# Attention's own-chunk products: 64x64 tiles on v where it stands, in place of 128x32 tiles on placed copies of v

## The reference, cut to what matters

```python
x = x + 0.5 * ffn(layernorm(x), w_gate, w_up, w_down)     # FP4 quantised, H=256, I=704
x = x + attn(layernorm(x), Wqkv, bqkv, Wout, bout, gamma, beta)
x = x + 0.5 * ffn(layernorm(x), w_gate, w_up, w_down)

# attn: linear attention, 16 heads of 16
q = (elu(q) + 1 + 1e-4) / sqrt(16);  k = elu(k) + 1 + 1e-4
num = einsum('blhe,blhef->blhf', q, cumsum_l(k v^T))
den = einsum('blhe,blhe->blh',   q, cumsum_l(k)) + 1e-4
out = layernorm((num / den) @ Wout.T + bout) * gamma + beta
```

## Time and profile before

| | |
|---|---|
| median of 3 runs | 2228.23 us |
| span of the profiled execution | 2226.0 us |
| PE busy | 2120.2 us, 95% |
| PEld busy | 1488.7 us, 67% |
| DVE busy | 2060.1 us, 93% |
| ACT busy | 1849.7 us, 83% |
| POOL busy | 1897.2 us, 85% |
| mean granted clock of TensorE | 0.994 of full speed |

### The profile page before, as it was taken

One profiled execution on the slowest core, in us unless ns is written; L12 is line 12 of the kernel. 1 busy time (PEld: TensorE's weight loads), 2 busy tenths in 40 slices (PEclk: granted clock), 3 DMA queues, 4 the chain that ended last, 5 costly groups with the idle time before them and its releaser, 6 DMA issues.

```text
span 2226.0 us, 90845 instructions
## 1 busy us (share of the span) xinstructions
PE 2120.2 (95%) x30384; PEld 1488.7 (67%) x30384; DVE 2060.1 (93%) x5231; ACT 1849.7 (83%) x3880; POOL 1897.2 (85%) x3002
## 2 busy tenths in 40 slices
PE   3899999999999899999999999969999999999998
PEld 1566666666666678888888888855656665666665
DVE  7999999999999689999999999978999999999997
ACT  7888888888888688888888888868888888888884
POOL 6899999999999677888888888868989999999996
PEclk9999999999999999999999999999999999999999
DMA  4765555555556433333333333324655555555555
GB/s 104 128 121 115 116 112 112 116 116 114 113 112 110 81 65 71 72 72 72 72 70 72 72 72 70 72 54 80 114 112 112 113 113 113 112 113 113 113 116 112
DMA packets 740337, 217.67 MB, mean 98 GB/s; under 512 B 670497, under 2 KB 740001, under 8 KB 740257
## 3 DMA queue, kind: packets, MB, share of 16 engines
q1 hardware_dynamic: 740256, 216.68, 48.2%
HBM read 20.38 MB, written 16.78 MB: 17 GB/s over the span
## 4 chain that ended last, share of the span: by engine, by line
DVE 38%; PE 20%; issue 12%; SPq 11%; POOL 11%; DMA 4%; DVEq 2%; ACT 1%; POOLq 0%; ACTq 0%
DVE ffn_y L748 10%; DVE ffn_per_block L717 8%; DVE ffn_hx L710 7%; PE ffn_ps_gu L860 6%; SPq L1028 5%; SPq L1034 4%; POOL ffn_h_hl L790 4%; POOL ffn_h_hl L791 4%; PE attn_ps_qk L1254 3%; DVE ffn_q L744 3%; PE ffn_ps_down L872 3%; DMA attn_xT<-attn_x_hl 3%; SPq L1040 2%; PE attn_ps_num L1293 2%; DVE ffn_scale L723 2%
## 5 line engine op out<-in xcount | busy, mean ns | idle before, releaser
L860 PE MATMUL ffn_ps_gu<-wgu_hi,ffn_xT 128*128 128x512 f16 (+1 forms) x3072 | 737.6, 363 | 17.7 <-DVE ffn_hx L710 7.5
L860 PEld LDWEIGHTS ffn_ps_gu<-wgu_hi,ffn_xT 128*128 128x128 f16 x3072 | 300.8, 98 | 303.6 <-issue 22.0
L806 ACT ACTIVATE ffn_quarter<-ffn_y,offsets 128x960 int16<-128x960 f32 (+2 forms) x264 | 282.6, 1071 | 185.0 <-DVE ffn_y L748 184.9
L860 PE MATMUL ffn_ps_gu<-wgu_lo,ffn_xT 128*128 128x512 f16 (+1 forms) x1536 | 431.0, 362 | 0.0
L872 PE MATMUL ffn_ps_down<-wd_hi,ffn_hT 128*128 128x256 f16 x2816 | 351.1, 273 | 18.9 <-DVE x_sb L737 13.6
L790 POOL TENSOR_TENSOR ffn_h_hl<-ffn_q,ffn_h_scale_hi 128x704 f16<-128x704 f16 x256 | 352.2, 1376 | 12.5 <-DVE ffn_h_scale_lo L754 8.4
L791 POOL TENSOR_TENSOR ffn_h_hl<-ffn_q,ffn_h_scale_lo 128x704 f16<-128x704 f16 x256 | 354.0, 1383 | 0.0
L872 PEld LDWEIGHTS ffn_ps_down<-wd_hi,ffn_hT 128*128 128x128 f16 x2816 | 265.7, 98 | 99.6 <-issue 37.0
L717 DVE TENSOR_REDUCE ffn_per_block<-ffn_hx 128x60 f32<-128x960 f32 (+2 forms) x264 | 298.4, 1130 | 21.3
L748 DVE TENSOR_TENSOR ffn_y<-ffn_hx,ffn_per_block 128x960 f32<-128x960 f32 (+2 forms) x264 | 295.3, 1119 | 0.0
L842 ACT ACTIVATE ffn_odd<-ffn_quarter,offsets 128x960 f16<-128x960 int16 (+2 forms) x264 | 278.7, 1056 | 10.5 <-POOL ffn_shift L783 10.5
(11 more groups left out here) (183 smaller groups left out, 5081.5 us busy)
## 6 DMA issues: line engine op xcount, KB each, us to landing
attn_v_eo<-attn_v_nat SPq DMA_DIRECT2D x512, 34.0 KB, 1.9
x_sb<-in_L_attn_x SPq DMA_DIRECT2D x128, 128.0 KB, 2.5
out<-x_sb SPq DMA_DIRECT2D x128, 128.0 KB, 2.1
ffn_xT<-ffn_x_hl SPq DMA_TRANSPOSE x256, 2.4
ffn_hT<-ffn_h_hl SPq DMA_TRANSPOSE x256, 3.5
attn_xT<-attn_x_hl SPq DMA_TRANSPOSE x128, 2.4
attn_oT<-attn_o_hl SPq DMA_TRANSPOSE x128, 2.4
x_sb<-in_L_ffn_w_gate SPq DMA_DIRECT2D x2, 352.0 KB, 5.0
```

The lines of the kernel that those rows point to most:

```text
L806: nc.scalar.activation(quarter[:, back], y[:, back], ACT.Identity, bias=offsets[:, 0:1], scale=4.0 / HALF_MIN).then_inc(S["quarter"], 1)
L860: last = nc.tensor.matmul(ps_gu[par][:, a:b], xT[par][:, c, :], w[:, k, a:b], start=(n == 0), stop=(n == len(terms) - 1))
```

## The change

The scores are now written with the keys of chunk s at the partitions half(s), where the v of that chunk stands, and even and odd heads lie side by side in the free dimension. The own-chunk product reads v where ScalarE wrote it: contraction over the 64 keys of chunk s, 64 columns of weights (all its queries), 17 moving columns (one head). Both operands and the output of chunk s lie at half(s), so chunk 0 uses the tile of the array at rows and columns 0 to 63, and chunk 1 that at rows and columns 64 to 127. There are again 32 such products per tile. `v_eo`, its four DMAs and all waits on them are gone. `v_nat` gets four buffers in place of two (hence a phase of 0 to 3 in place of the parity), and ScalarE no longer waits for a buffer of it to be free. The 32 products raise a new semaphore `own_done` at their last, and TensorE waits for it before the products with the state; that wait is new.

```diff
 def tensor_step(pe, i, phase):
...
                 ready(pe, "q_feat", tn)
-                placed(pe, tn, oth)
                 ready(pe, "masked", tn)
...
+                pe.sem_inc(S["turn"], 1)
                 for c in range(DC):
-                    for r in range(PAIRS):
-                        for u in range(4):
-                            s, m = u // 2, u % 2
-                            h = c * PAIRS + r % 2 * 2
-                            nc.tensor.matmul(num[quarter(u), r // 2, h:h + 2, :], scores[:, r // 2, c, s, r % 2, quarter(m)], v_eo[oth][:, s, :, c * PAIRS + r, :],
-                                             start=(c == 0 and r % 2 == 0), stop=False, skip_group_check=True)
+                    for g in range(2):
+                        for h in range(PAIRS):
+                            j, a = h // 2, h % 2
+                            for s in range(2):
+                                last = nc.tensor.matmul(num[half(s), g, c * PAIRS + h, :], scores[half(s), g, c, a, j, :], v_nat[(phase - 1) % PHASES][half(s), a, c * PAIRS + g * 2 + j, :],
+                                                        start=(c == 0 and h == 0), stop=False, skip_group_check=True)
+                last.then_inc(S["own_done"], 1)
+                ready(pe, "own_done", tn)
+                pe.sem_inc(S["turn"], 1)
...
-                                last = nc.tensor.matmul(ps_sc[half(a), g, c, s], k_eo[par][half(g), c, s, a], q_rows[par][half(g), c, :, half(s)], start=True, stop=True)
+                                last = nc.tensor.matmul(ps_sc[half(s), g, c, a], k_eo[par][half(g), c, s, a], q_rows[par][half(g), c, :, half(s)], start=True, stop=True)
...
 def sync_step(sp, i, phase):
...
-            if valid(tv, N):
-                ready(sp, "v_nat", tv)
-                sp.sem_inc(S["turn"], 1)
-                freed(sp, "num_done", tv, 2)
-                sp.sem_inc(S["turn"], 1)
-                for s in range(2):
-                    for a in range(2):
-                        sp.dma_start(v_eo[oth][half(a), s, a], v_nat[oth][half(s), a]).then_inc(S["v_eo" + even_odd], 16)
...
 def scalar_step(act, i, phase):
...
-                freed(act, "kv_done", tf, 2)
-                if not (isinstance(tf, int) and tf < 2):
-                    placed(act, tf - 2, oth)
-                nc.scalar.activation(v_nat[oth][:]...
+                nc.scalar.activation(v_nat[(phase + 1) % PHASES][:]...
```

More of the change, by code:

```diff
@@ L79 @@
 ATTN_TURN = 4
+PHASES = 4
 def in_order(eng, step, first, end):
     for i in range(first, end):
-        step(eng, i, i % 2)
+        step(eng, i, i % PHASES)
 def in_turns(eng, step, first, end, turn):
@@ L90, in in_turns @@
         for k in range(turn):
-            step(eng, i + k, (first + k) % 2)
+            step(eng, i + k, (first + k) % PHASES)
 FIRST, DEPTH = 12, 6
@@ L699, in sync_step, with vector_step @@
                 sp.dma_start(out_t[to], x_sb[:, to, :]).then_inc(stored, 16)
-        def vector_step(dve, i, par):
+        def vector_step(dve, i, phase):
+            par = phase % 2
             oth = 1 - par
@@ L878 @@
 ATTN_SEMS = ("sums", "stats", "var", "rstd", "shift", "xn", "x_hi", "x_split", "turn", "xT_even", "xT_odd", "qk_done", "relu", "exp", "feat", "k_even", "k_odd",
-             "q_feat", "q_rows", "v_done", "v_nat", "v_eo_even", "v_eo_odd", "kT_done", "k_nat", "scores_done", "masked", "kv_done", "kv_first", "kv_second",
-             "mid", "before", "num_done", "den", "rden", "o_ready", "o_hi", "o_split", "oT_even", "oT_odd", "proj_done",
+             "q_feat", "q_rows", "v_done", "v_nat", "kT_done", "k_nat", "scores_done", "masked", "kv_done", "kv_first", "kv_second",
+             "mid", "before", "own_done", "num_done", "den", "rden", "o_ready", "o_hi", "o_split", "oT_even", "oT_odd", "proj_done",
              "z_sums", "z_stats", "z_gamma", "x_beta", "consts", "w_turned")
@@ L920 @@
 ATTN_PLACES = {"o": 8352, "oT": (1024, 2048), "o_hl": (9376, 4096), "mid": (5632, 6176), "before": (6720, 7264), "first": 7808, "second": 11264, "k_nat": 12352, "zg": 13376,
-               "k_eo": (15104, 17152), "scores": 19200, "v_nat": (23296, 24384), "v_eo": (25472, 27648), "q_feat": (29824, 30848), "q_rows": (31872, 33920),
+               "k_eo": (15104, 17152), "scores": 19200, "v_nat": (23296, 24384, 27648, 28736), "q_feat": (29824, 30848), "q_rows": (31872, 33920),
                "expo": (35968, 38016), "xT": (40064, 41088), "x_hl": (42112, 43136), "xn": 44160,
@@ L952, in attention @@
         k_nat = sb("k_nat", [P, D])
-        v_nat = pair("v_nat", [P, 2, HEADS // 2, VW])
-        v_eo = pair("v_eo", [P, 2, 2, HEADS // 2, VW])
+        v_nat = [at(f"attn_v_nat{j}", ATTN_PLACES["v_nat"][j], [P, 2, HEADS // 2, VW]) for j in range(PHASES)]
         scores = sb("scores", [P, 2, DC, 2, 2, SUB])
@@ L988, in half @@
             return slice(s * SUB, (s + 1) * SUB)
-        def quarter(u):
-            return slice(u * SUB // 2, (u + 1) * SUB // 2)
         ps_kT, ps_v = ps_kT_first[:, 0:D], ps_v_second[:, 0:D]
@@ L1062, in vector_step @@
                 ready(dve, "scores_done", tm)
-                nc.vector.tensor_tensor(scores[:].rearrange("p g c s j q -> p (g c s j) q"), ps_sc[:].rearrange("p g c s j q -> p (g c s j) q"),
+                nc.vector.tensor_tensor(scores[:].rearrange("p g c a j q -> p (g c a j) q"), ps_sc[:].rearrange("p g c a j q -> p (g c a j) q"),
                                         causal[:].unsqueeze(1).to_broadcast([P, 4 * PAIRS, SUB]), ALU.mult).then_inc(S["masked"], 1)
@@ L1124, in gpsimd_step @@
                 pool.wait_ge(F["q"], N + X_AHEAD)
-                for j in range(2):
+                for j in range(PHASES):
                     nc.gpsimd.memset(v_nat[j][:], 1.0).then_inc(set_up, 1)
-                    nc.gpsimd.memset(v_eo[j][:], 0.0).then_inc(set_up, 1)
             if isinstance(i, int) and i == 1:
@@ L1319, in tensor_step @@
                             j = c * PAIRS + g * 2
-                            own_v = v_nat[par][half(s), :, j:j + 2, :].rearrange("p a j w -> p j a w")
+                            own_v = v_nat[phase][half(s), :, j:j + 2, :].rearrange("p a j w -> p j a w")
                             last = nc.tensor.matmul(half_state(s)[half(g), c * PAIRS * VW:(c + 1) * PAIRS * VW].rearrange("p (j a w) -> p j a w", a=2, w=VW),
```

45 lines of the change are left out of this document (26 added, 19 removed).

## The result

| | before | after |
|---|---|---|
| median | 2228.10 us (4 runs) | 2377.94 us (4 runs, 2376.27 to 2379.70) |
| ratio | | 1.0675, 95% interval 1.0662 to 1.0688 |
| span of the profiled execution | 2226.0 us | 2374.6 us, 148.6 more |
| PE busy | 95% | 96% |
| DVE busy | 93% | 86% |

The kernel became 150 us slower; the forecast was 134 slower, 2362 us. The page of after, against the earlier trace rows: busy times, slices, and the queues.

What follows compares the result with a forecast made beforehand. TensorE's own work, 5.42 of a 5.61 us attention step, was taken as the bound. Adding 1.30 gives 6.72: 112 x 1.11 + 16 x 0.65 = 134 us more, 2362 us; own range 2345 to 2390, 8-in-10 range 2255 to 2420.

Steps and rivals of the forecast that it cites:

- The pace of a pass: TensorE's own-chunk products: a 64-column load of 51 ns sets 55 ns a pass, 32 passes a tile, 1.76 us.
- The last product: End of the own-chunk group on TensorE: the last product takes 177 ns, scaled by 0.83 ns a column.
- The turn of the wait: TensorE's new wait for itself before the state products: 0.06 us from end to start, taken from VectorE's den.
- The sum: First own product to first state product: 1.76 + 0.18 + 0.06 = 2.00 us, 1.30 more than now.
- the step of 5.42: Attention step before the change in which TensorE hardly waits: 5.42 of 5.61 us taken as TensorE's own work.
- the 16 steps at the ends: Attention steps between FFN steps, where TensorE rests: half of the 1.30 us counted, 0.65 each, 10 us.
- What goes: Four DMAs leave SyncE's queue, 2.38 us of its step; all 0.19 us a step of TensorE's waits counted as removed.
- The count of passes (2): Own-chunk products: number of passes counts, not shape; 9 ns each, 0.11 us more a step, kernel 2219 us. Chance 0.12.
- a load at the strips' price (3): Own-chunk products: a load costs 25 ns, 28 a pass; 0.44 us more a step, kernel 2259 us. Chance 0.13.
- no overlap (4): Own-chunk products: load and product in a tile don't overlap, 69 ns a pass; 1.75 us more, kernel 2417. Chance 0.07.
- Rival 2: Own-chunk products: passes cost 9 ns each whatever their shape, so the kernel gets 9 us faster, 2219 us. Chance 0.12.
- The clock: TensorE's clock stays at 1.00; should it fall to the lower level in the sparse stretch, the forecast is too low.

Runs made afterwards that it cites:

- e3: The changed kernel with the 32 own-chunk products dealt over four 64x64 tiles in place of two, their order changed, sums landing elsewhere: 2267.21 us.
- e2: The changed kernel with 34 moving columns in each own-chunk product in place of 17, num being another sum: 2379.55 us.
- e12: The changed kernel with 68 moving columns in each own-chunk product in place of 17, num being another sum: 2386.68 us.
- e1: The kernel before, without the four copies of v on SyncE and the waits on them, so num lacks its own-chunk part: 2215.28 us.
- e4: The changed kernel with a second wait of TensorE for itself, after 16 of the 32 own-chunk products: 2460.88 us.
- e8: The changed kernel with attention's loop written over 8 steps in place of 4, the same work in the same order: 2498.04 us.

## Why the prediction was right

**The views.** TensorE's own step was read as the bound, with VectorE next at 5.3 us. After the change VectorE is at 330.76 / 65.6 = 5.0 us a step and waits for the rest, so all of TensorE's loss counted. That is 0.24 less than the 5.28 of before, for the same 14 instructions a step: the one that adds to `x_sb` takes 568 ns in place of 726 and the one that makes `before` 322 in place of 398, in the same shapes. Why they got shorter is open. It is one reason why den waits 1.77 us a step and not the 1.4 forecast.

**The pace of a pass** was the term on which all hung: 55 ns forecast, from 51 ns of load. Measured by the difference of e3 and after it is 57, from the group's row (2.04 - 0.21) / 31 = 59. The last product starts 1.83 us after the first and not 1.76, so in the sum this makes 0.07 us. The Trainium skill, TensorE: Matmul & The Clock Gate, LDWEIGHTS, gives columns / 1.2 in ns for a load, by which 64 columns are an estimate of 53 ns; the pace here lies about a tenth over it.

**The last product** was 177 ns by scaling with its columns, and is 207. With 34 and 68 columns (e2, e12) the medians of such products are 221 and 217: at this pace the durations hardly follow the columns, and scaling by 0.83 ns a column didn't hold. 0.03 us.

**The turn of the wait** was taken from VectorE's den, 0.06 us. TensorE's wait for itself takes 0.15, from the end at 1015.05 to the start at 1015.20. 0.09 us. This was the largest relative error: the price was taken from a row of another engine.

**The sum.** These three make 0.19 us: 2.19 to 2.20 in place of 2.00. The rest of the step came out at 6.86 - 2.20 = 4.66 in place of 5.42 - 0.70 = 4.72; perhaps the step of 5.42 still held a little waiting. That it took back part of the three errors is luck. So the step is 6.86, not 6.72, and 112 steps give 112 x (6.86 - 5.61) = 140 us, not 124. The remaining 9 of 148.6 us are put down to the 16 steps at the ends, 0.5 each; 0.65 was counted.

**What goes.** The 0.19 us a step of waits did vanish in after, as counted. But the reason given, a queue with room, is only half of it: e1 has the room too, and its loads keep 13.1 of the 19.7 us of waits for xT. In after they vanish, and the likely reason is that TensorE's longer step gives xT 1.25 us more time; that was not tried by itself.

**The rivals.** The count of passes (2) is refuted by e3; a load at the strips' price (3) by the group's 59 ns; no overlap (4) by e12. Rival 2 had a true core: the strips of before start a record every 9 ns, so nothing common to all products holds them further apart. It erred in holding that for 64-column loads on two tiles. The prediction's own reason against it, the 51 ns of a load that nothing covers, decided.

**The clock**, named as what could spoil the forecast, stayed at 1.00 in the middle of the stage. e4 shows how near it was: with one more stop a step it fell in some of the steps.

## What to carry to other kernels

Many small float32 products cost their weight loads: count the passes of the busiest tile of the array times the pace for that width of load (here 57 to 59 ns at 64 columns, 35 to 49 at 32), and ask how many tiles work side by side before asking how many products there are. A copy that allows a contraction over all 128 partitions on four strips can be cheaper than products on the data where it stands, as long as its DMAs are nearly hidden: here the copies cost 13 us and the products without them 150. And before taking work off a queue, look at what its next entry waits for: if that is data and not the queue, little comes sooner.

## What had not been expected of the hardware

- The length of a loop body has a price of its own: 3.59 MB of instructions fetched in place of 0.66, stops such as those of 2.95 and 2.67 us among the first products of a step, and 120 us in all for the same work (e8).
- The clock can fall though TensorE hardly rests: in e4 it fell after two microseconds in which the engine was busy for 0.84 and 0.85, small products with two stops of 0.16 us. The step before had the same stretch and kept 1.00. What sets it off was not settled.
- A self-wait of TensorE costs 0.33 us a time (e4): 0.16 of turn, and the end of a last product over which nothing else lies.
